# A gated graph network on one core: r times hn is put into the n gate's PSUM bank and TensorE adds the product on the sums onto it; the last layer's low h is divided at column 350

## The reference, cut to what matters

```python
for l in range(4):
    m = x @ weight[l]
    agg = segment_sum(m[src], dst)           # the loops add x's own row
    gi = agg @ w_ih.T + b_ih;  gh = x @ w_hh.T + b_hh
    r = sigmoid(i_r + h_r);  z = sigmoid(i_z + h_z)
    n = tanh(i_n + r * h_n)
    x = (1 - z) * n + z * x
out = layernorm(2 * x0 + x)
```

## Time and profile before

| | |
|---|---|
| median of 3 runs | 2330.45 us (2329.63 to 2331.1) |
| span of the profiled execution | 2327.4 us, 3.05 us under that median |
| busy in the span | TensorE 2229.5 us (96%), VectorE 2175.6 (93%), ScalarE 1842.3 (79%), GpSimd 1719.4 (74%) |
| chain that ended last | TensorE 66%, VectorE 18%, issue 10%, ScalarE 2%, DMA 2%, GpSimd 1% |
| TensorE's granted clock | 0.986 of full speed on average, 0.99 to 1.00 after the first 80 us |

### The profile page before, as it was taken

The page is one execution under the profiler, slowest core; times in us unless marked ns, Lnnn a source line. Parts: engine busy times, 40 slices in busy tenths (PEclk is TensorE's granted clock), DMA queues, the critical chain, the costliest instruction groups (busy, mean ns, idle before and its releaser), DMA issues.

```text
span 2327.4 us, 49180 instructions
## 1 busy us (share of the span) xinstructions
PE 2229.5 (96%) x11728; PEld 1898.3 (82%) x11728; DVE 2175.6 (93%) x4211; ACT 1842.3 (79%) x3483; POOL 1719.4 (74%) x1654
## 2 busy tenths in 40 slices
PE   3999999999999999999999999999989999999996
PEld 2888888888878888888878888888877888888885
DVE  7899999999879999999969999999969999999998
ACT  1688888888768888888857888888856888888886
POOL 3877777777487777777558777777748888888884
PEclk7999999999999999999999999999999999999998
DMA  2455555555545555555545555555544555555554
GB/s 58 120 155 160 158 160 161 158 160 160 157 131 173 171 173 172 174 172 173 166 127 172 172 171 172 173 174 171 174 130 122 159 156 155 155 155 154 155 155 118
DMA packets 277064, 362.45 MB, mean 156 GB/s; under 512 B 107754, under 2 KB 186586, under 8 KB 276980
## 3 DMA queue, kind: packets, MB, share of 16 engines
q1 hardware_dynamic: 238118, 309.12, 43.5%
q0 software_dynamic: 38784, 52.30, 9.7%
q10 hardware_dynamic: 78, 0.08, 0.0%
HBM read 208.71 MB, written 179.20 MB: 167 GB/s over the span
## 4 chain that ended last, share of the span: by engine, by line
PE 66%; DVE 18%; issue 10%; ACT 2%; DMA 2%; POOL 1%; DVEq 1%; SPq 0%; ACTq 0%; POOLq 0%
PE pZ L847 17%; PE pR L847 8%; PE pHN L847 8%; PE pA L835 8%; PE pO L929 5%; PE pIN L847 4%; PE pA L847 4%; DVE bn L1442 3%; PE pR L891 3%; PE pR L888 3%; PE pR L889 3%; DVE diff L1411 3%; DVE aggT L1381 3%; DVE y_rows L1435 2%; PE pH L786 2%
## 5 line engine op out<-in xcount | busy, mean ns | idle before, releaser
L683 POOL DMA_INDIRECT gath<-state,idx x900 | 931.4, 1035 | 264.6 <-issue 255.8
L660 POOL TENSOR_TENSOR h_lo<-hT,h_hi 128x500 fp32r<-128x500 f32 (+1 forms) x400 | 375.8, 940 | 200.5 <-ACT h_hi L1050 149.7
L683 POOL DMA_INDIRECT gath<-in_x_dram,idx x300 | 321.9, 1073 | 101.8 <-issue 68.7
L1080 ACT ACTIVATE rg<-pR,bsum 128x500 f32<-128x500 f32 x400 | 269.7, 674 | 112.2 <-PE pR L891 100.2
L1400 DVE SCALAR_TENSOR_TENSOR narg<-pHN,bhh,rg 128x500 f32<-128x500 f32 x400 | 292.3, 731 | 44.9 <-ACT rg L1080 44.1
L1372 DVE TENSOR_TENSOR a_lo<-aggT,a_hi 128x500 fp32r<-128x500 f32 x396 | 271.5, 686 | 0.3
L1062 ACT CAST sel<-sel 128x504 fp32r (+1 forms) x400 | 245.9, 615 | 31.6 <-DVE flag_i L1356 29.5
L1417 DVE TENSOR_TENSOR diff<-pZ,diff 128x500 f32<-128x500 f32 x400 | 267.7, 669 | 0.8
L1381 DVE TENSOR_TENSOR aggT<-pA,hT 128x500 f32<-128x500 f32 x396 | 263.8, 666 | 1.7 <-PE pA L835 1.6
L1088 ACT ACTIVATE pZ<-pZ,bsum 128x500 f32<-128x500 f32 x400 | 256.1, 640 | 0.0
L1067 ACT CAST a_hi<-aggT 128x500 fp32r<-128x500 f32 x396 | 235.6, 595 | 6.5 <-DVE aggT L1381 6.5
(11 more groups left out here) (211 smaller groups left out, 6384.1 us busy)
## 6 DMA issues: line engine op xcount, KB each, us to landing
columns<-newT SPq DMA_DIRECT2D x300, 250.0 KB, 2.3
hT<-columns SPq DMA_DIRECT2D x300, 250.0 KB, 2.7
state<-o_rows SPq DMA_DIRECT2D x300, 224.0 KB
x_rows<-in_x_dram SPq DMA_DIRECT2D x200, 224.0 KB
out_dram<-o_rows SPq DMA_DIRECT2D x91, 224.0 KB
gath<-state,idx POOLq DMA_INDIRECT x900, 2.4
state<-o_rows SPq DMA_DIRECT2D x297, 26.0 KB
idx<-edge_src SPq DMA_DIRECT2D x395, 1.5 KB
```

Of the source, the lines that this page charges most:

```text
L660: nc.gpsimd.tensor_tensor(part_of(h_lo, u)[:, cols], hT[:, u % RING, cols], part_of(h_hi, u)[:, cols].bitcast(F32), ALU.subtract).then_inc ...
L683: pool.indirect_dma_start(out=gath[:, u % RING, j, :], out_offset=None, in_=states[l], in_offset=bass.IndirectOffsetOnAxis(ap=idx[:, u % R ...
L1080: nc.scalar.activation(rg[:, :], pR[:, 0:COLS], ACT.Sigmoid, bias=bsum[:, 0:1]).then_inc(s_r, 1)
```

## The change

`r_times_hn_below_in` writes r times hn (with its bias) into `n_bank(u)` instead of `narg`. TensorE then adds the product on the sums onto that bank (`n_onto_r_times_hn`, no start flag), at the end of its step behind turn_back, and in a layer's last step behind z. `n_argument` goes, and tanh is done within the bank (`n_gate_in_place`). The first four blocks of a layer (`ADDED_APART`) keep the old way. With that, the orders change: tanh, difference and product of block b-1 stand at the beginning of step b on ScalarE and VectorE, new_state(b-1) behind them and ahead of r times hn(b); high_h and part 0 of the normalising stand ahead of the r gate (part 0 in every fifth step behind it). `LOW_BY_POOL` replaces `HALF` and `halved`: in the last layer GpSimd makes 350 columns of low h and VectorE the other 150; before, GpSimd made all 500. The core of the diff:

```diff
-HALF = COLS // 2
+LOW_BY_POOL = COLS, COLS // 2, COLS // 2, 350
+ADDED_APART = RAMP
+        def shared(l):
+            return LOW_BY_POOL[l] < COLS
+        def seeded(i, u):
+            return not (isinstance(i, int) and i == 0 and u < ADDED_APART)
...
-                cols = slice(0, COLS if whole or not halved(l) else HALF)
+                cols = slice(0, COLS if whole else LOW_BY_POOL[l])
...
+            def n_onto_r_times_hn(l, b, u):
+                pe.wait_ge(s_t1, l * NB + b + 1)
+                product(l, u, n_bank(u), 2, ("in",), False, True, True).then_inc(s_IN, 1)
...
-                        n_on_sums(l, b, u, l * NB + b - 1 if l or exists_before(i, u, 2) else None)
+                        if not onto:
+                            n_on_sums(l, b, u, l * NB + b - 1 if l or exists_before(i, u, 2) else None)
...
+                        if last:
+                            n_onto_r_times_hn(l, b, u)
                         if not first:
                             pb, pu, _ = after(i, u, -1)
                             turn_back(l, pb, pu, isinstance(i, int) and pb == 0,
...
+                        if onto and not last:
+                            n_onto_r_times_hn(l, b, u)
...
+            def n_gate_in_place(l, b, u):
+                act.wait_ge(s_IN, l * NB + b + 1)
+                nc.scalar.activation(n_bank(u), n_bank(u), ACT.Tanh, bias=bih[:, 2:3]).then_inc(s_n, 1)
...
+                        if exists_before(i, u, ADDED_APART + 1):
+                            n_gate_in_place(l, *after(i, u, -1)[:2])
                         if not ramp:
                             rows(i, u)
+                            high()
+                        fresh = half_done(i, u, OUTLAG) if final else None
+                        if not fresh:
+                            normal(i, u, 0)
                         r_gate(l, b, u, first and l == 0)
+                        if fresh:
+                            normal(i, u, 0)
...
-                        normal(i, u, 0)
...
-                        n_gate(l, b, u)
+                        if not seeded(i, u):
+                            n_gate(u, l * ADDED_APART + b + 1)
...
+            def r_times_hn_below_in(l, b, u):
+                g = l * NB + b
+                dve.wait_ge(s_HN, g + 1)
+                dve.wait_ge(s_r, g + 1)
+                v.scalar_tensor_tensor(n_bank(u), pHN[:, 0:COLS], bhh[:, 2:3], rg[:, :],
                                        ALU.add, ALU.mult).then_inc(s_t1, 1)
...
+                        if exists_before(i, u, ADDED_APART + 1):
+                            difference(l, *after(i, u, -1)[:2])
+                            product(l, *after(i, u, -1)[:2])
+                        if onto or u:
                             renew(*after(i, u, -1))
...
-                        r_times_hn(l, b, u)
+                        if onto:
+                            r_times_hn_below_in(l, b, u)
+                        else:
+                            r_times_hn(l, b, u)
+                            n_argument(l, b, u)
                         if shifted:
                             shift(*shifted)
-                        if not ramp and not last:
-                            renew(*after(i, u, -1))
-                        n_argument(l, b, u)
...
-                        difference(l, b, u)
+                        if not onto:
+                            difference(l, b, u)
...
-                        coming = coming if coming and halved(coming[0]) else None
+                        coming = coming if coming and shared(coming[0]) else None
...
-                        product(l, b, u)
+                        if not onto:
+                            product(l, b, u)
...
                         if last:
+                            difference(l, b, u)
+                            product(l, b, u)
                             renew(b, u, i)
```

More of the change, by code:

```diff
@@ L836, in sum_edges, with product @@
                 last.then_inc(s_pA, 1)
-            def product(l, u, bank, c, sides, begins=True, ends=True):
+            def product(l, u, bank, c, sides, begins=True, ends=True, onto=False):
                 passes = []
@@ L847, in product @@
                     last = nc.tensor.matmul(bank, w, xx, start=begins and k == 0,
-                                            stop=ends and k == len(passes) - 1)
+                                            stop=ends and k == len(passes) - 1, skip_group_check=onto)
                 return last
@@ L938, in step @@
                         ramp = isinstance(i, int) and i == 0 and u < RAMP
-                        r_on_state(l, b, u, start, halved(l))
+                        onto = seeded(i, u)
+                        r_on_state(l, b, u, start, shared(l))
                         if not start:
@@ L1151, in step, with high @@
                         ramp = isinstance(i, int) and i == 0 and u < RAMP
+                        coming = on_from(l, i, u, PRE)
+                        def high():
+                            if coming:
+                                nl, nb, nu, ni = coming
+                                high_h(nl, nb, nu, TURNS * (nl - 1) + turn(ni, nu) + 1)
+                        if exists_before(i, u, ADDED_APART + 1):
+                            n_gate_in_place(l, *after(i, u, -1)[:2])
                         if not ramp:
                             rows(i, u)
+                            high()
+                        fresh = half_done(i, u, OUTLAG) if final else None
+                        if not fresh:
+                            normal(i, u, 0)
                         r_gate(l, b, u, first and l == 0)
+                        if fresh:
+                            normal(i, u, 0)
                         if ramp:
@@ L1158, in step @@
                             rows(i, u)
[L1159 to L1167, removed]
+                            high()
+                        if coming and coming[0] == l and not ramp and not final:
+                            if not opening(i):
+                                high_gathered(l, *coming[1:3], turn(*coming[:1:-1]))
+                            widen(l, *coming[1:3])
                         if ramp and u == 1:
@@ L1189, in fast_path @@
                     blocks(act, step)
+                    n_gate_in_place(l, NB - 1, UNROLL - 1)
                     for k in range(lag, 0, -1):
@@ L1364, in low_h @@
                 dve.wait_ge(s_hhi, l * NB + b + 1)
[L1365 to L1366 removed]
+                cols = slice(LOW_BY_POOL[l], COLS)
+                v.tensor_tensor(part_of(h_lo, u)[:, cols], hT[:, u % RING, cols],
+                                part_of(h_hi, u)[:, cols].bitcast(F32), ALU.subtract).then_inc(s_hlov, 1)
             def low_part(l, b, u, summed=False):
@@ L1400, in r_times_hn @@
                 v.scalar_tensor_tensor(narg[:, :], pHN[:, 0:COLS], bhh[:, 2:3], rg[:, :],
+                                       ALU.add, ALU.mult).then_inc(s_t1, 1)
+            def r_times_hn_below_in(l, b, u):
[3 more added lines that the diff above has]
+                v.scalar_tensor_tensor(n_bank(u), pHN[:, 0:COLS], bhh[:, 2:3], rg[:, :],
                                        ALU.add, ALU.mult).then_inc(s_t1, 1)
@@ L1502, in step @@
                         ramp = isinstance(i, int) and i == 0 and u < RAMP
-                        if last:
-                            renew(*after(i, u, -1))
-                        if ramp and u:
+                        onto = seeded(i, u)
+                        if exists_before(i, u, ADDED_APART + 1):
+                            difference(l, *after(i, u, -1)[:2])
+                            product(l, *after(i, u, -1)[:2])
+                        if onto or u:
                             renew(*after(i, u, -1))
```

9 lines of the change are left out of this document (3 added, 6 removed).

## The result

The changed kernel takes 2386.85 us (median of 4 runs, 2384.12 to 2389.03), the kernel before in the same job 2330.77 us (4 runs): 1.0238 times as long, 95% interval 1.0223 to 1.0252. The forecast was 2386.8 us. The profiled execution's span is 2387.2 us, against 2327.4 before; the mean granted clock is 0.988 of full speed against 0.986, so the clock is no part of it.

A forecast was written before the change was run, and what follows sets the result against it. TensorE was taken to bound layers 0 to 2, VectorE the last. Changes of +11 (layers 1 and 2), +43 (last layer) and +2 us (ends, openings) gave 2386.8 us; range for 8 in 10: 2348 to 2403 us.

The forecast's parts named there:

- the ring: Tanh, difference, product, new state, r times hn, addition, high part, z gate, next tanh: 5.28 us a block, layers 1 and 2.
- One sign that the forecast named: In layers 1 and 2 TensorE would no longer be busy all the time.
- the old 5.216: Block period of layers 1 and 2 before the change, in us, taken as TensorE's own work.
- Dependent neighbours: VectorE instructions waiting for the one in front: difference to product 0.78 us, product to new state 0.81 us.
- Rival A: Dependence on VectorE costs less, 0.71 us for both spacings; ring 5.11 us, whole kernel 2357 us; chance 0.12.
- rival B: VectorE's dependent instructions spaced as independent ones, 0.59 us; kernel 2330 to 2337, say 2333 us, no change; chance 0.08.
- The rest of the ring: Hops after new state: 0.60, 0.64, 0.67, 0.04, 0.50 and 0.57 us, plus 0.67 from tanh to difference.
- The last layer: Two normalising instructions lengthen the ring to 6.05 us; two odd blocks in five make 6.27 a block, +43 us.
- VectorE's own sum: VectorE's work per last-layer block: 5.73 us, below the ring's 6.05; 6.36 in the block with the moments.
- openings: First blocks of the layers: gathered high part between z gate and tanh in three blocks, about +1 us in all.
- The ends: Layer ends, where n_onto follows z's six matmuls: 0 to 0.7 us later, taken as 0.3, +1.2 us for four layers.
- the way over TensorE: Return path through z, transposes, n_onto and tanh, about 0.3 us shorter than through high part and z gate, so not deciding.

The follow-up runs named there:

- e4: Changed kernel with the low part of the gathered rows (0.47 us) moved ahead of VectorE's addition in layers 0 to 2: 2484.93 us, 1.066.
- e5: Changed kernel with ScalarE's high part of the next block moved behind tanh and VectorE's low part behind product: 2328.37 us, 0.9987.
- e7: Kernel before with two more, long fulfilled waits ahead of the last layer's row statistics: 2332.01 us, 1.0007.
- e9: Changed kernel with product's and new state's waits, except for the instruction in front, moved ahead of the difference: 2365.66 us, 1.0147.
- e12: Changed kernel, unchanged, profiled a second time: span 2384.5 us, one run.
- e8: Changed kernel, high part and shift moved earlier; in the last layer low part between difference and product, low h between product and new state: 2318.54 us, 0.9947.
- e11: Changed kernel with e8's moves, last layer's second normalising part ahead of the z gate, and 300 instead of 350 columns of low h by GpSimd: 2305.01 us, 0.9887.

## Why the prediction was right, and where only its sum was

Right, step by step:
- **Which ring.** The high part waits for the addition in every block (81 of 82), e4 makes the ring longer and pays for all of it, e5 opens it and gets TensorE's bound back. In layer 0, with 5.63, it does not decide until e4 brings it to 5.77. One sign that the forecast named did not come: TensorE still counts as busy all the time, and only its count of matmuls shows the gaps. Nor was the old 5.216 TensorE's own work to the last hundredth, as the forecast read it: e5 does the same work in 5.19. What the other 0.026 us were is open.
- **Dependent neighbours.** Difference to product 0.78 as forecast, product to new state 0.78 in 45 blocks of layer 1's loop and 0.81 in 37, 0.80 on average (0.81 forecast). This was the term that divided the forecast from the rivals A and B, and rows from a layer's end carried over to the loop. Rival A's thought, that the waits make 0.78 out of 0.71, is right as a mechanism (e7, e9): it is the wait that has become an instruction between the neighbours. It changes nothing in the time, since this code has such an instruction there.
- **The rest of the ring.** New state to r times hn 0.59 (0.60), to the addition 0.65 (0.64), addition 0.67 and 0.03 to the high part, then 0.51 (0.50), 0.57, tanh 0.64 and 0.03 to 0.04. Sum 5.28.
- **The last layer.** Five blocks (difference to difference, from 2000.09) took 6.03, 6.39, 6.02, 6.83 and 6.03, together 31.30; forecast 31.35. Over the whole stretch the mean is 6.293 (6.265 in e12); forecast 6.27. The 6.39 (2006.12 to 2012.51) is VectorE's own sum; in the 6.83 the normalising waits 1.96 us for shift (2021.56, released by the instruction at 2021.33), and the high part starts at 2022.85, 4.33 us behind the difference, as forecast.

Mis-sized terms. From the first r gate of a layer to its last, in us:

| | layer 0 | layer 1 | layer 2 | last | between layers, start and tail |
|---|---|---|---|---|---|
| measured, after minus before | -0.7 | +7.0 | +8.2 | +46.9 | -1.6 |
| forecast | 0 | +5.6 | +5.6 | +43 | +1.2, openings +1 |

Together they make +59.8 in the profiled execution, against the forecast's +56.4. The ends were given +0.3 each for n_onto behind z; from layer 1 to 2 the gap even fell by 1.8 us. The last layer's opening was given a part of +1; its first ten steps took 63.24 us against 58.58. By e12, where they take 61.11, some 2 us of these 4.7 are one execution's long instructions, and about 2.5 belong to the change. Layer 2's period is 5.294 instead of 5.28, which is 1.2 of its 2.6 us beyond the forecast: in eight of 81 blocks product to new state takes 0.90 to 1.14 instead of 0.78, in e12 too, and why is open. Of the other 1.4 there, and of the 1.4 in layer 1, 0.9 each lie in a layer's first ten steps (56.99 against 56.07 us in layer 1); e12 has 55.88 there, so that much differs from one execution to the next. The medians lie 56.1 us apart, 3.7 less than the two profiled executions. So the mechanism and the large terms were right, but that the total came within 0.1 us of the measured median is luck. The sum was 3.4 us short of the profiled pair (6.9 us too little in layers 1, 2 and the last, 0.7 and 2.8 too much in layer 0 and in what lies between), and the profiled pair is 3.7 us wider than the medians. The forecast's own spread was not added up right either: +-0.04 on the ring over 264 blocks is +-10.6 us, 2376 to 2397, not 2373 to 2400; nothing hangs on it.

One argument left out a way that mattered later. The forecast weighed the way over TensorE by n_onto and tanh, about 0.3 us shorter than the ring; the one by z's matmuls, the z gate and ScalarE's queue it did not price. In e8's plain blocks the product starts 1.18 us behind the difference (2012.14 to 2013.32) instead of 0.78, and that second way is the bound.

The rule of the Trainium skill ("VectorE: DVE Perf Modes", The DRAIN you can't avoid), by which semaphores in a chain cost nothing, would have given rival B's 2333 us. The page measured it on a chain of copies; for neighbours of which one waits for the other the runs disagree: 0.59 for independent neighbours, 0.71 with the one wait for the instruction in front, 0.78 to 0.81 with more. Another page of the Trainium skill, "Perfetto Trace Analysis", Identifying Dependency Chains, says that an instruction which waits for several engines can get semaphore instructions of its own ahead of it; the traces agree. They show `EVENT_SEMAPHORE` between the neighbours wherever these stand at 0.76 or more, and none where they stand at 0.71 (e9, e7's loop). Why it costs 0.07 to 0.10 us while it is shown with 0.02 to 0.05 is open. Two such instructions also lie between new state and r times hn (906.8 and 907.0), and there the spacing stays 0.59: they run while new state still does.

## What to carry to other kernels

Follow the order of the in-order queues around, from one block to the same place in the next: if an instruction that everything waits for stands behind one that waits for it, the chain is a ring, and its sum, not the busiest engine, is the period. Price each hop from starts of neighbours with the same dependence in the trace (0.59 independent, 0.71 to 0.81 dependent here, the upper values where a wait has become an instruction between the two), and look for the ring's second way, since work moved out of one is easily moved into the other. An instruction saved on an engine that is not the bound (n_argument, 0.59 us a block) is worth nothing, while the order that it takes to save it cost 35 to 50 us; the same saving with the ring opened gained 1.1% together with a new place for shift, low parts and normalising and a new split (e11).

## What the runs showed that was not expected

- A wait can cost even when it is long fulfilled, and what it costs depends on where its instruction comes to stand: two more took residual to row statistics from 0.71 to 0.81 us in written-out steps, where it stands between the two, and nothing in the loop, where it has run before (e7). Put ahead of an instruction that stalls anyway, waits delay its start from 0.03 to 0.13 us behind its release (e9).
- VectorE writing to PSUM instead of SBUF takes as long: r times hn 0.74 us against 0.73, and the next starts 0.65 behind it against 0.64.
- Single VectorE instructions took 1.0 to 1.75 us instead of 0.2 to 0.67 in the last layer's opening, some in one execution only, some at the same block in two kernels, and the kernel before has them too. Their cause is open.
